# Four block entries of an eight-stage decoder kernel: order of maxima, statistics, queries and counts

## The reference

```
attention (a1, a2, a3): q = ln(x) @ Wq + bq;  k, v from the context;  16 heads of 8
    a2 turns q and k by positions first (rotary);  scores = q.k * scale, softmax over 64 keys
    x = x + (softmax @ v) @ Wo + bo
f3:  p = softmax(ln(x) @ gate.T)              8 experts
     choose the 2 largest of p + gate_bias;  weights are p of the chosen
     x = x + sum_e weight_e * w2_e(silu(w1_e h) * w3_e h) + shared(h)
```

## Time and profile before

| what | us |
|---|---|
| runs | 1155.78, 1159.92, 1160.05 (median 1159.92) |
| the profiled execution | 1160.51 |
| its span, first to last instruction | 1158.7 |
| busy in the span: PE, DVE, ACT, POOL | 945.0, 835.1, 648.0, 465.2 |
| chain that ended last, by engine | PE 34%, DVE 28%, issue 8%, ACT 4%, POOL 3% |

### The profile page before, as it was taken

How to read it: one execution, slowest core, us unless ns; L and a number is a source line. 1 busy time by engine, 2 the same in 40 slices (tenths; PEclk the granted TensorE clock), 3 DMA queues, 4 the chain that set the end, 5 groups by cost and what they waited for, 6 DMA issues and landing times.

```text
span 1158.7 us, 21041 instructions
## 1 busy us (share of the span) xinstructions
PE 945.0 (82%) x7166; PEld 635.6 (55%) x7166; DVE 835.1 (72%) x2078; ACT 648.0 (56%) x1143; POOL 465.2 (40%) x446
## 2 busy tenths in 40 slices
PE   5868810478987999789879999998988997957997
PEld 3653310454545677345445666665654556536996
DVE  6786699866887675467888999999847885622443
ACT  4424567955653345556558778785646654213553
POOL 5500000001220001435469999998311233473555
PEclk9888965688999999899988999999979998987999
DMA  8000000037000000000000000000000000024431
GB/s 290 1 1 1 1 0 0 1 119 227 2 1 1 1 1 2 1 2 1 2 1 1 2 0 0 0 0 1 1 1 2 1 2 1 27 104 116 113 103 34
DMA packets 24233, 33.76 MB, mean 29 GB/s; under 512 B 3484, under 2 KB 20389, under 8 KB 23888
## 3 DMA queue, kind: packets, MB, share of 16 engines
q1 hardware_dynamic: 20720, 26.20, 7.4%
q0 software_dynamic: 3424, 6.38, 1.6%
HBM read 18.34 MB, written 15.98 MB: 30 GB/s over the span
## 4 chain that ended last, share of the span: by engine, by line
PE 34%; DVE 28%; issue 8%; ACT 4%; POOL 3%; DVEq 0%; DMA 0%; POOLq 0%; ACTq 0%
DVE big L850 7%; DVE hq L845 7%; PE psum L619 5%; PE psum L2540 5%; PE psum L1602 3%; POOL rows L2410 3%; DVE big L2199 2%; PE psum L2556 2%; ACT psum L2048 2%; PE psum L573 2%; PE psum L1619 2%; DVE big L854 2%; DVE tmp L1838 1%; DVE psum L1838 1%; DVE psum L1850 1%
## 5 line engine op out<-in xcount | busy, mean ns | idle before, releaser
L845 DVE TENSOR_REDUCE hq<-psum 128x16 f32<-128x1024 f32 x96 | 114.6, 1221 | 83.4 <-PE psum L573 45.5
L2122 POOL TENSOR_TENSOR big<-big 128x512 f32<-128x512 f32 x128 | 128.6, 1043 | 7.0 <-ACT big L1878 7.0
L2048 ACT ACTIVATE psum<-big,tmp 128x512 f32<-128x512 f32 x128 | 85.0, 686 | 19.5 <-DVE big L2199 16.9
L2199 DVE SCALAR_TENSOR_TENSOR big<-big,tmp,psum 128x512 f32<-128x512 f32 x128 | 90.4, 744 | 4.5 <-ACT psum L2048 1.3
L735 ACT ACTIVATE big<-psum 128x1024 f32<-128x1024 f32 x64 | 62.0, 1021 | 54.7 <-PE psum L603 54.7
L2727 DVE SCALAR_TENSOR_TENSOR big<-psum,big 128x128 f32<-128x128 f32 x118 | 36.0, 348 | 72.6 <-issue 44.0
L850 DVE RECIPROCAL big<-psum 128x256 f32<-128x256 f32 x48 | 84.0, 1750 | 5.2 <-PE psum L619 4.9
L483 POOL TENSOR_TENSOR big<-big,w_const 128x256 f32<-128x256 f32 x32 | 24.0, 750 | 153.4 <-PE psum L619 146.0
L1516 PE MATMUL psum<-f_downT,tmp 128*128 128x128 f32 x192 | 25.2, 296 | 68.0 <-DVE tmp L1399 68.0
L2132 POOL TENSOR_TENSOR big<-big 128x1024 f32<-128x1024 f32 x32 | 75.2, 2361 | 12.0 <-DVE big L2199 12.0
L2420 POOL DMA_INDIRECT out<-big x59 | 57.9, 982 | 50.6 <-issue 29.8
(11 more groups left out here) (336 smaller groups left out, 2638.5 us busy)
## 6 DMA issues: line engine op xcount, KB each, us to landing
rows<-pad SPq DMA_DIRECT2D x1, 7670.0 KB, 33.5
big<-rows SPq DMA_DIRECT2D x59, 130.0 KB, 2.1
tmp<-in_pack_f SPq DMA_DIRECT2D x1, 2050.5 KB, 9.6
w_f<-in_pack_f SPq DMA_DIRECT2D x1, 1280.0 KB, 12.4
tmp<-in_pack_once SPq DMA_DIRECT2D x1, 960.0 KB, 7.0
out<-big POOLq DMA_INDIRECT x59
X<-in_x SPq DMA_DIRECT2D x1, 768.0 KB, 5.2
w_a<-in_pack_a SPq DMA_DIRECT2D x3, 256.0 KB, 7.9
```

The costliest lines, as they stand in the source:

```text
L845: dve.tensor_reduce(nm, psum[:, 1 + 2 * t:3 + 2 * t, :].rearrange("p c (r l k) -> p (c r) l k", r=2, k=SK), AX.X, ALU.max, negate=True).th ...
L2048: act.activation(bank(EX_BANK + h % 2), ssum[t][:, h * 512:(h + 1) * 512], ACT.Exp, bias=shift2[:, t * NH2 + h:t * NH2 + h + 1]).then_inc( ...
L2122: ins = pool.tensor_tensor(ssum[t][:, h * 512:(h + 1) * 512].rearrange("p (i j) -> p i j", i=ROWS2), st[:, 0, h, 0:ROWS2].unsqueeze(2).to_ ...
L2199: dve.scalar_tensor_tensor(out=ew[t][:, blk], in0=ssum[t][:, blk], scalar=best2[:, t, h, 7:8], in1=bank(EX_BANK + h % 2), op0=ALU.is_ge, o ...
```

## The change

It does the following. `residual` can leave its statistics out, so that they are issued later. At the entries of a2 and a3 DVE takes the four maxima of items 0 and 1 before the last group's statistics and variance; at a1 the second two are issued before the last residual itself. At a2 the queries 2 and 3 and their copies go in between the maxima, and the turn of group 2 behind ST(0), its copy between the two exponentials. In all three, MX(2, 1) goes ahead of the next query. In f3, `counts`, `firsts` and `places` are issued earlier on PE, the places and POOL's wait for them are split in two halves of 16 tiles, gate columns and add(0) change place on DVE, several small operands move from SBUF to PSUM bank 5, and five matmuls whose result nobody uses stand ahead of the block loop, released when POOL has come to its last sends but one.

```diff
@@ residual
-        def residual(dve, s, g, src, last_sub, ready):
+        def residual(dve, s, g, src, last_sub, ready, stats_too=True):
...
-            tail_stats(dve, s, g, last_sub)
+            if stats_too:
+                tail_stats(dve, s, g, last_sub)
@@ heads_pe
-            for b in range(2, L.ahead):
-                Q(b)
-            for b in range(2 - L.ahead, 0):
-                turn_ahead(b)
+            if not L.rope:
+                Q(2)
             for b in range(B + 2):
                 if b < B:
                     ST(b)
+                if b == 0:
+                    for k in range(2 - L.ahead, 0):
+                        turn_ahead(k)
...
                 if b + 1 < B:
                     NM(b + 1)
+                if b == 0:
+                    MX(2, 1)
                 if b + L.ahead < B:
                     Q(b + L.ahead)
-                if b + 2 < B:
+                if b and b + 2 < B:
                     MX(b + 2, 1)
@@ heads_act
-            for b in range(2, L.ahead):
-                takeQ(b)
+            takeQ(3 if L.rope else 2)
             if L.rope:
                 rotated16(2)
-            for b in range(2 - L.ahead, 0):
-                take_ahead(b)
...
                 exp(b, 0)
+                if b == 0:
+                    for k in range(2 - L.ahead, 0):
+                        take_ahead(k)
                 exp(b, 1)
@@ f0_dve
+                if g == N_GROUPS - 1:
+                    a1.mx(1, 0)
+                    a1.mx(1, 1)
                 residual(dve, s, g, bank(7 - g % 2), False, (S("f0_o_ps"), g + 1))
...
-                if g >= 6:
-                    a1.mx(g - 6, 0)
-                    a1.mx(g - 6, 1)
+                if g == N_GROUPS - 2:
+                    a1.mx(0, 0)
+                    a1.mx(0, 1)
@@ f0_pe
+            a1.MX(1, 0)
             a1.T(1)
-            a1.MX(1, 0)
             a1.NM(0)
             a1.MX(1, 1)
@@ f1_pe
             a2.MX(0, 0)
+            a2.T(1)
             a2.MX(0, 1)
-            a2.T(1)
+            a2.Q(2)
             a2.MX(1, 0)
             a2.NM(0)
             a2.MX(1, 1)
+            a2.Q(3)
@@ f1_act
             a2.rotated16(0)
+            take_turned(act, "a2", 1, 1)
             a2.rotated16(1)
-            take_turned(act, "a2", 1, 1)
+            a2.takeQ(2)
             a2.takeN(0)
@@ f1_dve, and f2_dve in the same way
             res(N_GROUPS - 1)
-            stats_done(dve, s, "a2", 1)
-            ln_var_dve(dve, "a2", 1)
             for b in range(2):
                 a2.mx(b, 0)
                 a2.mx(b, 1)
+            tail_stats(dve, s, N_GROUPS - 1, False)
+            stats_done(dve, s, "a2", 1)
+            ln_var_dve(dve, "a2", 1)
@@ f3_pool
-            pool.wait_ge(S("f3_m"), 5)
...
             for t in range(N_TILES):
+                if t % 16 == 0:
+                    pool.wait_ge(S("f3_m"), 5 + t // 16)
+                if t == N_TILES - 2:
+                    pool.sem_inc(S("f3_near"), 1)
@@ f3_pe, order (places waits for D3, and for the block table only ahead of its second half)
             down(0)
+            counts()
             up(2, 0)
+            firsts()
             up(2, 1)
-            counts()
+            places()
             down(1)
-            firsts()
             up(3, 0)
-            places()
             up(3, 1)
             down(2)
...
-            pe.wait_ge(S("f3_m"), 6)
+            pe.wait_ge(S("f3_m"), 7)
             pe.wait_ge(S("f3_x"), N_GROUPS)
+            pe.wait_ge(S("f3_near"), 1)
+            for _ in range(5):
+                pe.matmul(bank(3)[:, 0:2 * P], ident, W["f3_s1"], start=True, stop=True)
@@ gates (mx3, eq3[0], which3[0], pid3 become mxp, eqp, firstp, pidp in bank 5)
+                eqp = bank(5)[:, 256:512].rearrange("p (t e) -> p t e", e=E3)
+                mxp, firstp, pidp = (bank(5)[:, 32 * i:32 * i + 32] for i in range(3))
...
-                    step(dve.tensor_tensor(eq3[0], eq3[0], rev, ALU.mult))
+                    step(dve.tensor_tensor(eqp, eqp, rev, ALU.mult))
@@ f3_dve
             gates()
+            gate_column(0, lo3)
...
+            base3 = bank(5)[:, 128:128 + N_TILES]
...
-            gate_column(0, lo3)
+            add(0)
             gate_column(1, hi3)
-            add(0)
-            dve.wait_ge(S("f3_lg"), N_GROUPS + 3)
             for h in range(2):
+                half = slice(16 * h, 16 * h + 16)
+                dve.wait_ge(S("f3_lg"), N_GROUPS + 3 + h)
...
-            dve.tensor_copy(place3, place3f).then_inc(S("f3_m"), 1)
+                dve.tensor_copy(place3[:, half], place3f[:, half]).then_inc(S("f3_m"), 1)
```

More of the change, by code:

```diff
@@ L1729, in res @@
             def res(g):
-                residual(dve, s, g, bank(7), False, (S("f1_val"), 4 * g + 4))
+                residual(dve, s, g, bank(7), False, (S("f1_val"), 4 * g + 4), g < N_GROUPS - 1)
             def body(g, j):
@@ L2267, in body @@
                     a3.keys16(1)
-                residual(dve, s, g, bank(7), False, (S("f2_o_ps"), 4 * g + 4))
+                residual(dve, s, g, bank(7), False, (S("f2_o_ps"), 4 * g + 4), one_more)
             groups2(dve, body)
-            stats_done(dve, s, "a3", 1)
-            ln_var_dve(dve, "a3", 1)
             for b in range(2):
@@ L2275, in f2_dve @@
                 a3.mx(b, 1)
+            tail_stats(dve, s, N_GROUPS - 1, False)
+            stats_done(dve, s, "a3", 1)
+            ln_var_dve(dve, "a3", 1)
         rowbuf = big[:, 2 * HALF - N_TILES * ROW3 - 512:2 * HALF - 512].rearrange("p (t n) -> p t n", n=ROW3)
@@ L2294, in build @@
         eq3 = [f3.take(N_TILES * E3).rearrange("p (t e) -> p t e", e=E3) for _ in range(2)]
-        which3 = [f3.take(N_TILES) for _ in range(2)]
-        mx3, sum3, rec3, lo3, hi3, pid3, place3f = (f3.take(N_TILES) for _ in range(7))
+        mx3, second3, sum3, rec3, lo3, hi3, place3f = (f3.take(N_TILES) for _ in range(7))
         place3 = f3.take(N_TILES).bitcast(U32)
@@ L2301, in build @@
         pre3 = [f3.take(16 + N_TILES + 1) for _ in range(2)]
-        base3 = f3.take(N_TILES)
         nb3, st3, en3, st128 = (f3.take(2) for _ in range(4))
@@ L2470, in places @@
             def places():
-                pe.wait_ge(S("f3_m"), 4)
-                pe.matmul(bank(6)[0:1, 448:508], W["f3_lohi"][0:PAIRS3, :], oh3[0:PAIRS3, :], start=True, stop=True)
                 for h in range(2):
+                    if h:
+                        pe.wait_ge(S("f3_m"), 4)
+                        pe.matmul(bank(6)[0:1, 448:508], W["f3_lohi"][0:PAIRS3, :], oh3[0:PAIRS3, :], start=True, stop=True)
+                    else:
+                        pe.wait_ge(S("f3_m"), 3)
                     pe.matmul(bank(5 + h)[:, 0:16 * PAIRS3], tri16,
@@ L2480, in places @@
                                     start=False, stop=True, skip_group_check=True)
-                ins.then_inc(S("f3_lg"), 1)
+                    ins.then_inc(S("f3_lg"), 1)
             up(0, 0)
@@ L2689, in f3_dve @@
             dve.wait_ge(S("f3_m"), 2)
-            step(dve.tensor_tensor(en3[K, 0:1], st3[K, 0:1], nb3[K, 0:1], ALU.add))
+            step(dve.tensor_tensor(en3[K, 0:1], bank(6)[K, 480:481], nb3[K, 0:1], ALU.add))
             step(dve.tensor_scalar(ge3[K, :], W["f3_blk"][K, :], st3[K, 0:1], None, ALU.is_ge))
@@ L2693, in f3_dve @@
                                      op0=ALU.is_lt, op1=ALU.mult).then_inc(S("f3_m"), 1)
-            gate_column(0, lo3)
+            add(0)
             gate_column(1, hi3)
-            add(0)
-            dve.wait_ge(S("f3_lg"), N_GROUPS + 3)
             for h in range(2):
-                step(dve.tensor_tensor(pm3[h], M3[:, 16 * h:16 * h + 16, :],
+                half = slice(16 * h, 16 * h + 16)
+                dve.wait_ge(S("f3_lg"), N_GROUPS + 3 + h)
+                step(dve.tensor_tensor(pm3[h], M3[:, half, :],
                                        bank(5 + h)[:, 0:16 * PAIRS3].rearrange("p (t k) -> p t k", k=PAIRS3), ALU.mult))
-                step(dve.tensor_reduce(place3f[:, 16 * h:16 * h + 16], pm3[h], AX.X, ALU.add))
-            dve.tensor_copy(place3, place3f).then_inc(S("f3_m"), 1)
+                step(dve.tensor_reduce(place3f[:, half], pm3[h], AX.X, ALU.add))
+                dve.tensor_copy(place3[:, half], place3f[:, half]).then_inc(S("f3_m"), 1)
             add(1)
```

24 lines of the change are left out of this document (12 added, 12 removed).

## The result

The kernel after takes 1139.62 us (median of 4, 1138.48 to 1140.14) against 1159.99 (1155.78 to 1160.75) for the kernel before in the same session: a ratio of 0.9829, 95% interval 0.9807 to 0.985. The profiled execution of after took 1140.14 (span 1138.4), that of before 1160.51 (1158.7), so the traces differ by 20.3 us, and 19.1 were forecast.

What follows compares the result with a forecast made beforehand. The prediction took the chain of waits as the bound (PE on 34%, DVE on 28%). Its terms, 1.1 + 1.1 + 9.3 + 5.9 + 1.7 = 19.1, off 1160.51 gave 1141.4, stated as 1141 us, range 1137 to 1145.

Steps and rivals of the forecast that it cites:

- signs of being wrong: Last stage and blocks: DVE's wait for counts was to be under 1 us, the first two blocks at full clock.
- a2, 9.3: Entry of a2: statistics behind four maxima, queries among them, ST(0) before T(2); 9.3 us gained, bounds 6.5 and 10.
- a1 and a3, 1.1 each: Entries of a1 and a3: ST(0) starts 1.4 us earlier, 0.3 charged against it, net 1.1 us gained in each.
- the charge for what comes behind ST(0): a1 and a3: Q(3)'s copy, group 2's turn and ST(1) queue behind MX(2,1); 0.3 us lost in each.
- rival (a): a1 and a3: the clock does not fall there, worth 3 us each, total 1135; chance 25%.
- The 0.3 for MX(2,1) ahead of Q(3): a1 and a3 entries: MX(2,1) takes 0.61 us ahead of Q(3); charged 0.3 us, bounds 0 and 0.6.
- Last stage, 5.9: Up to the first send: counts 3.4, gate_column(0) in the wait 1.37, halves 1.3 less 0.1; sum 5.9 us gained.
- Counts: Last stage: moved ahead of up(2,0), DVE's copy of the counts comes at 990.7 instead of 994.10, 3.4 us gained.
- the halves: Last stage: per-half places let POOL start after one half, 1.3 us gained less 0.1 for second cast and waits.
- Scratch in PSUM, 0: Gates of the last stage: they may end 0.95 us earlier, but that buys nothing; 0, bounds -0.3 and +1.
- Matmuls before the blocks, 1.7: Before the block loop: five matmuls begin with the last sends but one, first blocks at full clock; 1.7 us gained.
- Rival (c): Last stage: sends wait for adds that come 3 us later, 1.7 of 5.9 lost, 1143 or 1145; chance 9%.

Runs made afterwards that it cites:

- e11: The kernel after with MX(2,1) behind Q(3) again in a1 and a3, a2 unchanged; 1138.0 us in a single run.
- e1: The kernel before with the a2 entry's edits alone, MX(2,1) ahead of the next query in a2 only; ratio to before 0.992.
- e2: The kernel before with the a1 and a3 entries' edits alone; ratio to before 0.9921.
- e8: The kernel after with the gates' scratch and base3 in SBUF again instead of PSUM; ratio to before 0.9847.
- e5: The kernel after with ten matmuls before the blocks instead of five, released by the landing of row send 26; ratio to before 0.9807.
- e7: The kernel after with an extra memset of 128x1024 on POOL behind its last product, ahead of the first send's waits; 1145.34 us in a single run.
- e12: The kernel after with ten matmuls released by send 26's landing, hid(2,1) on DVE, and POOL's wait for the places first; ratio to before 0.9835.
- e4: The kernel after without the five matmuls before the blocks and without their semaphore; ratio to before 0.982.

## Why the prediction was right, and where it was not

The time was right (1141 forecast, 1139.62 measured), and at a2, the largest term, by the mechanism given. That the total came so close is in part luck. Of the 20.3 us, 1.15 lie ahead of a1's entry and 1.1 ahead of the gates, where no code that runs there changed, and 0.8 come from a clock that rose early; they about make up for a2's dip and for matmuls that missed. Two of my own signs of being wrong did show: the granted clock was half in the first blocks, and DVE waited 1.43 for the counts, not under 1. Point by point:

- *a2, 9.3: right at the entry.* ST(1) came 8.8 sooner net of what a1 carried in (forecast 9.3 to 9.6); most of the difference is the 0.59 that DVE stands for MX(1,0), which I had not charged. At the end of the stage after keeps 7.6 of it, since the clock falls to half once; alone, in one trace without that dip, the edit gave 10.4. My line that 7.1 us of before "hold no maximum" was a misreading: the fourth ran at 469.09, and ST(0) came 5.8 after its end. The statistics were held a little beside POOL (L224, L225 and L230 took 0.67 to 0.76 instead of 0.17), and no maximum was late for it.
- *a1 and a3, 1.1 each: too small in a1.* The step that failed is the charge for what comes behind ST(0). I let the clock fall as in before; counted from the first MX it fell about 3 us later and came back about 3 us earlier. ST(0) gained its 1.5, ST(0) to ST(1) went from 7.96 to 6.55 and ST(1) to ST(2) from 7.79 to 7.57, so rival (a) held in part: 3.2 for a1. In a3 ST(0) came 1.46 sooner behind the residual; the stretch gained 0.7 in after and 2.2 in six of the others. The 0.3 for MX(2,1) ahead of Q(3) is 0 (e11).
- *Dips.* My forecast adds its terms, as if a stretch at half clock stayed where it was. e1, e2 and after show that it does not: of 14.2 us in the three edited stretches, 11.5 to 13.0 are left when the edits stand together, and a2's dip takes 2.8 in after.
- *Last stage, 5.9: right in its sum (5.7), wrong in its parts.* Counts arrived 3.9 sooner (3.4), the halves 1.4 (1.3). Not foreseen: 0.83 that gate_column(1) loses beside POOL's product, 0.7 for the order of POOL's waits, and as much in its favour from the five steps of the scan (1.75 us beside a product of POOL in before, 1.05 in after).
- *Scratch in PSUM, 0: the term that failed.* I read L2629's 898 ns as a thing of the gates alone and argued that the gates' end buys nothing. But once the counts stand directly behind M3, a late M3 makes PE wait (2.10 in e8), and moving them forward puts D3, which ran clear in before (1.08), beside a product of POOL. Without the scratch the same reordering gives 1.4, not 5.7 (27.69 to 26.29), and 0.9 against e2's 27.17. Most of what I counted as the reordering's gain rests on the edit that I counted as nothing. The Trainium skill (SBUF — State Buffer, Who interferes with whom) has the rule: a DVE instruction with two SBUF inputs and a GpSimd instruction that reads SBUF exclude each other for the whole instruction. e8's rows agree, with 0.95 to 1.04 lost each time. Beside it I had put the longer fixed part of PSUM sources (the Trainium skill, VectorE: DVE Perf Modes, The TRN2 errata), about 0.065 us by my estimate; 0.43 against 0.42 says that here it is 0.01 at most.
- *Matmuls before the blocks, 1.7: place wrong, size borne out by one trace.* "They begin with the last sends but one" took the semaphore increment for a part of the sends' order. It ran by 1013.7, while the engine was at send 21 (counted from 0) and the increment stood ahead of send 30: eight sends were still to come before it. The Trainium skill (Advanced Engine Details and Errata, Engine Queue Depths) gives GpSimd a queue of 8, which agrees. Held by a landing, they gave 1.7 to 2.4 in one trace (e5).
- *Rival (c)* was judged by slack on the trace shown, and did not come true there (sends unbroken). On two of the four chips the sends did wait for adds, by 3.9 to 6.8 us. But e1 and e2, with the old order, lose 4.1 there too, so it is mostly not the reordering of up and down that I had named, but the standstills of DVE and ACT below.

## What to carry to other kernels

When a phase is moved forward, look at what it will then lie beside and what it will then wait for: the cost of e8 is in steps that nobody moved on purpose and in a wait that had not mattered, and one operand in PSUM removed both. A semaphore increment in POOL's list can fire ahead of the work that stands before it, here by eight sends, 10 us; to time something by a DMA, let the DMA's own completion release it. Gains of single entries are not to be added to better than a few microseconds where the clock dips: e1 has 2.6 us of scatter in a stage whose code did not change.

## What the runs showed of the hardware that I had not expected

The clock also fell while PE was busy without a gap. In e7 (and e12), ahead of the gates, PE is busy 4.00 of 4.00 us in three windows on end, and in the second the clock begins to fall, in the third it is at half; the gates start 4 us later than in e5, where PE was as busy and the clock stayed at 1.00 up to 960. What tells the two apart is not shown. Windows of e7:

```profile
952.00:956.00 4.00, 4.00 (x22) 2.56 (x21) 2.88 (x18) 2.28 (x7) 0.08 (x1) 1.00 0.00 0
956.00:960.00 4.00, 4.00 (x35) 4.00 (x34) 0.73 (x6) 2.48 (x5) 0.00 (x0) 0.87 0.00 0
960.00:964.00 4.00, 4.00 (x21) 4.00 (x21) 0.00 (x0) 0.61 (x2) 0.00 (x0) 0.50 0.00 0
```

On two of four chips DVE and ACT stand for 3 to 12 us during the sends and in e1 to e4 the two start again within 0.1 us of each other. In e1, DVE and ACT:

```profile
1015.05 0.69 DVE L2669 TENSOR_TENSOR big<-X,psum 128x512 f32<-128x512 f32 x1 [11.47 <-remote]
```

```profile
1015.09 1.08 ACT L2573 ACTIVATE big<-psum 128x512 f32<-128x512 f32 x2 [12.23 <-remote]
```

The kernel before is 9 to 10 us slower on those chips; by the traces of e1 and e2 about 4 of it is in the sends and 4 in the blocks. That the two engines resume together suggests a cause common to them; none was tested, and it stays open.
